# Attention over graph edges with a software gather: dropping implied semaphore waits, building the one-hot tile before the clip, and copying the edge rows after the query rows

## What is computed

```python
Q_h = (x @ Wq + bq).reshape(N, H, D)
K_h = (x @ Wk + bk).reshape(N, H, D)
V_h = (x @ Wv + bv).reshape(N, H, D)
E = (edge_attr @ We + be).reshape(-1, H, D)
score = K_h[src] * Q_h[dst] / sqrt(D) * E
score = exp(clip(score.sum(-1, keepdims=True), -5.0, 5.0))
wV = segment_sum(V_h[src] * score, dst)
Z  = segment_sum(score, dst)
out = layernorm(x + (wV / (Z + 1e-6)).reshape(N, H * D))
```

## Time and profile before

| | |
|---|---|
| median of three runs | 1276.63 us (1275.21 to 1278.20) |
| profiled execution, own time | 1267.1 us |
| its span | 1265.2 us |
| mean granted TensorE clock | 0.723 of full speed |
| busy: POOL, PE, PE weight load, DVE, ACT | 758.5, 694.1, 477.0, 620.3, 180.9 us |
| indirect DMAs of line 377 | 750, 0.97 us each |

### The profile page before, as it was taken

The page is one execution under the profiler, slowest core; times in us unless marked ns, Lnnn a source line. Parts: engine busy times, 40 slices in busy tenths (PEclk is TensorE's granted clock), DMA queues, the critical chain, the costliest instruction groups (busy, mean ns, idle before and its releaser), DMA issues.

```text
span 1265.2 us, 11863 instructions
## 1 busy us (share of the span) xinstructions
PE 694.1 (55%) x3376; PEld 477.0 (38%) x3376; DVE 620.3 (49%) x1205; ACT 180.9 (14%) x343; POOL 758.5 (60%) x788
## 2 busy tenths in 40 slices
PE   4655646454445446436585575575545555565554
PEld 4554333243234324324353333343324333343332
DVE  1221435454355346436594554554545544544556
ACT  1224201111011011101120110110111110110111
POOL 7371456666656656656536566666666666666660
PEclk8657767768667767767796776677676786687777
DMA  7464254354355345444455445445435454454440
GB/s 185 156 198 139 79 149 128 102 158 130 105 142 139 106 127 150 115 125 127 135 144 146 125 114 157 127 115 156 126 105 164 129 140 133 127 135 135 121 115 28
DMA packets 89940, 165.51 MB, mean 131 GB/s; under 512 B 43315, under 2 KB 61908, under 8 KB 86840
## 3 DMA queue, kind: packets, MB, share of 16 engines
q1 hardware_dynamic: 52843, 89.34, 25.6%
q0 software_dynamic: 37024, 75.35, 21.4%
HBM read 152.22 MB, written 12.39 MB: 130 GB/s over the span
## 4 chain that ended last, share of the span: by engine, by line
another core or an unknown queue 40%; PE 21%; issue 17%; DVE 13%; ACT 6%; DMA 2%; SPq 0%; DVEq 0%
PE psE L434 7%; DVE qe L786 5%; ACT qe L601 5%; PE psA L496 4%; PE psT L451 4%; DVE logit L875 2%; DMA xt<-xT 1%; DVE msg L890 1%; PE psQ L416 1%; DVE qke L866 1%; PE psA L461 1%; PE psE L404 1%; DVE clipped L881 1%; DVE ob L838 1%
## 5 line engine op out<-in xcount | busy, mean ns | idle before, releaser
L377 POOL DMA_INDIRECT kv<-kv_table,idx x750 | 726.7, 969 | 468.7 <-issue 221.4
L496 PE MATMUL psA<-place,msg 128*104 128x104 f32 x1564 | 210.4, 301 | 289.9 <-DVE msg L890 220.6
L496 PEld LDWEIGHTS psA<-place,msg 128*104 128x104 f32 x1564 | 198.5, 213 | 318.6 <-DVE msg L890 235.0
L434 PE MATMUL psE<-ea,we 97*96 97x512 f32 x392 | 256.3, 790 | 0.0
L774 DVE TENSOR_TENSOR place<-psI,rel_tile 128x832 f32<-128x832 f32 (+1 forms) x99 | 98.5, 995 | 293.9 <-remote 293.9
L451 PE MATMUL psT<-identity,qe 96*128 96x96 f32 x782 | 114.7, 307 | 153.0 <-DVE qe L786 124.0
L601 ACT ACTIVATE qe<-psE 96x1024 f32<-96x1024 f32 (+1 forms) x99 | 99.9, 1009 | 622.0 <-remote 469.4
L786 DVE TENSOR_TENSOR qe<-psQ,qe 96x1024 f32<-96x1024 f32 (+1 forms) x99 | 119.1, 1203 | 82.3 <-ACT qe L601 33.8
L451 PEld LDWEIGHTS psT<-identity,qe 96*128 96x128 f32 x782 | 96.9, 181 | 165.1 <-DVE qe L786 128.3
L866 DVE TENSOR_TENSOR qke<-psT,kv 128x768 f32<-128x768 f32 (+1 forms) x99 | 92.9, 938 | 87.6 <-remote 86.9
L434 PEld LDWEIGHTS psE<-ea,we 97*96 97x96 f32 x392 | 75.8, 218 | 79.3 <-issue 79.3
(11 more groups left out here) (107 smaller groups left out, 356.8 us busy)
## 6 DMA issues: line engine op xcount, KB each, us to landing
ea<-eaT SPq DMA_DIRECT2D x49, 768.0 KB
q_parts<-rel_table SPq DMA_DIRECT2D x24, 1008.0 KB
kv<-kv_table,idx POOLq DMA_INDIRECT x750
qwin<-q_table SPq DMA_DIRECT2D x198, 23.6 KB
xb<-xrows SPq DMA_DIRECT2D x24, 144.0 KB
out<-ob SPq DMA_DIRECT2D x24, 144.0 KB
q_table<-q_parts SPq DMA_DIRECT2D x4, 720.0 KB
kv_table<-kv SPq DMA_DIRECT2D x2, 960.0 KB
```

The source lines that it names most:

```text
L377: pool.indirect_dma_start(kv[:, k, t], None, kv_table, sources).then_inc(kv_in[k], 16)
L434: last = nc.tensor.matmul(psE[0:D, h, 0:size], we[:], ea[:, k // 2 % 2, edge:edge + size], start=True, stop=True)
L496: last = nc.tensor.matmul(psA[0:ML, off:off + PW], msg[:, s, t], place[:, s, t], start=opens, stop=closes)
```

## The change

All edits are inside `edge_pass`. The semaphore `e_done` goes. ACT's copy of `psE` waits for `q_done` of the group in place of `e_done` (and of `t_done`). Waits are dropped on PE (`qe_done` ahead of `to_edges`, and `ea_in` for the second group of a pair), on ACT (`t_done`, `sum_done`) and on DVE (`q_done` in `make_pick` and `make_qe`, `wt_done` before the clip, `sum_done` before `msg`, `rel_in` for three groups of four). `make_place` of g+1, which stood behind the clip of g, now stands ahead of it, behind `between(1)`; its own wait for `sum_done` of g-1 stays.

```diff
                         g = U * r + k
                         spans_of = [...]
-                        pe.wait_ge(ea_in[k // 2 % 2], 16 * lap(r, k, 4))
-                        if at >= 1:
-                            pe.wait_ge(qe_done, g)
+                        if k % 2 == 0:
+                            pe.wait_ge(ea_in[k // 2 % 2], 16 * lap(r, k, 4))
                         for h, size in spans_of:
                             edge = (k % 2) * GE + h * GE // 2
-                            last = nc.tensor.matmul(
+                            nc.tensor.matmul(
                                 psE[0:D, h, 0:size], we[:], ea[...], start=True, stop=True)
-                        last.then_inc(e_done, 1)
                         pe.wait_ge(qwin_in[k % QRING], 32 * lap(r, k, QRING))
...
-                        act.wait_ge(e_done, g + 1)
-                        if at >= 2:
-                            act.wait_ge(t_done, g - 1)
+                        act.wait_ge(q_done, g + 1)
                         nc.scalar.activation(qe[...], psE[...], ACT.Copy).then_inc(e_up, 1)
...
                             act.wait_ge(clip_done, g + 1)
                             nt = tiles(at)
-                            if at >= 2:
-                                act.wait_ge(sum_done, g - 1)
                             nc.scalar.activation(msg[...], clipped[...], ACT.Exp).then_inc(wt_done, 1)
...
-                        g = U * r + k
-                        dve.wait_ge(rel_in[k // BG % 2], 16 * (r + k // U + 1))
-                        if at >= 2:
-                            dve.wait_ge(q_done, g - 1)
+                        if k % BG == 0:
+                            dve.wait_ge(rel_in[k // BG % 2], 16 * (r + k // U + 1))
                         nc.vector.tensor_scalar(pick[...], rel[...], query_id[0:QR], None,
...
-                        dve.wait_ge(q_done, g + 1)
                         dve.wait_ge(e_up, g + 1)
                         nc.vector.tensor_tensor(qe[...], psQ[...], qe[...], ALU.mult).then_inc(qe_done, 1)
...
                         between(1)
-                        if at >= 2:
-                            dve.wait_ge(wt_done, g - 1)
+                        if at + 1 < NG:
+                            make_place(r, k + 1, at + 1)
                         dve.wait_ge(logit_done, g + 1)
                         nc.vector.tensor_scalar(clipped[...], logit[...], -5.0, 5.0, ALU.max,
                                                 ALU.min).then_inc(clip_done, 1)
                         between(2)
-                        if at + 1 < NG:
-                            make_place(r, k + 1, at + 1)
                         between(3)
-                        if at >= 2:
-                            dve.wait_ge(sum_done, g - 1)
                         dve.wait_ge(wt_done, g + 1)
                         nc.vector.tensor_tensor(msg[...], kv[...], msg[...], ALU.mult).then_inc(msg_done, 1)
```

More of the change, by code:

```diff
@@ L174, in gnn_program @@
         window_up, acc_out = sem("window_up"), sem("acc_out")
-        e_done, q_done, sum_done = sem("e_done"), sem("q_done"), sem("sum_done")
+        q_done, sum_done = sem("q_done"), sem("sum_done")
         pick_done, place_done = sem("pick_done"), sem("place_done")
```

## The result

The changed kernel takes 1288.29 us (median of six, 1285.34 to 1293.68), the kernel before 1277.47 us (six, 1275.21 to 1281.24). The ratio is 1.0088, 95% interval 1.0062 to 1.0115: slower by 11 us. Forecast were 1290 us. The profiled execution of the changed kernel took 1293.7 us by its own time and is the slowest of its six; that of before, with 1267.1 us, lies under all six of its own. Between the two profiles lie 26.6 us, of which less than half is the change.

The account below looks back on a forecast made before the run. POOL's gathers and stops were taken to bound the kernel. Terms of 10.2, 0.6, 1.2 and 1.0 us gave 13.0 us slower, 1289.7 us by the median (prediction 1290); range 1253 to 1303, the main forecast's own 1284 to 1303.

Parts of the forecast that it names:

- What bounds the kernel: POOL's gathers: 10.2 us a group of eight, compute under 6; only what lengthens or shortens POOL's stops moves the end.
- the forecast's floor: POOL's gathers without stops: 91 groups behind the ring's first eight take 928 us of the 1267.
- `place` ahead of the clip: At POOL's stops, clip and exponential come between release and `msg`: 17 stops at 0.6 us, 10.2 us slower.
- The number of stops: POOL's stops behind `msg`, 205 to 616 us: stay at 16, growing from 4.46 to about 5.1 us each.
- The waits at zero: Dropped waits on PE, ACT and DVE: records lie beside work, taken as 0, at most 0.6 us gain.
- the copy at zero: ACT's copy behind the query rows: 0.4 to 0.8 us later, hidden behind POOL or the burst, taken as 0.
- Behind group 48: 23 stops waiting for `q_done`: DVE's new order adds nothing, taken as 0, upper bound 14 us.
- The tail: Behind the last gather: three small groups lose the exponential's cover, about 1 us slower.
- The standstill: 630 to 652 us, POOL still and DVE full: four groups lose the exponential's cover, 1.2 us slower.
- Rival B: PE posts a quarter fewer signals, so POOL's stops shorten by 37 us: 1253 us, faster; chance 0.26.
- Rival D: Copy waiting for `q_done` is caught by holds, 3.1 us a stop, in half the stops: 1350 us; chance 0.11.

Follow-up runs that it names:

- h1: Kernel before with only the one-hot tile of the next group built ahead of the clip, on a chip with holds: 1301.86 us, ratio 1.0148.
- h2: Changed kernel with the one-hot tile put back behind the clip, on a chip with holds: 1304.21 us, ratio 1.0111 to the kernel before.
- c2: Kernel before without the implied waits, copy still on `e_done`, tile behind the clip, on a chip with holds: 1286.56 us, ratio 1.0106.
- the earlier limit: Kernel before with POOL's extra wait for `q_done` from group 12 on instead of 48, on a chip with holds: 1258.99 us, ratio 0.9881.

## Why the prediction was right, and where it wasn't

*What bounds the kernel: right.* POOL's pace and its stops. On the chip without holds the stops are gone and the time is 1056 us; the forecast's floor is what is left (group 8 starts at 107 us in the run with the tile alone, 928 us later POOL's last gather ends, at 1035).

*`place` ahead of the clip: mechanism and price right, its share wrong.* I put 17 stops at 0.6 us. (The count leaves out the stop of the earlier trace rows, whose gather at 619.41 lies behind the window; it should have been 18.) Measured are 0.51 us (1.45 against 0.94), and 0.8 where a longer step of the block lies between, as at 243.63 to 245.37. But only ten of the 14 stops in the first stretch are not of the new kind. They last 5.12 us on average in place of 4.46, as forecast (about 5.1), and account for 6.6 of the 18.5 us by which POOL's stops grew there. Four of the new kind, 9.67 us with the issue, account for 20.9, and two stops fewer give 8.9 back. I didn't have this part in this form.

*The number of stops: the failed step.* I wrote that I'd be wrong if it changed. It did, from 16 to 14, in the first stretch, with 24 gathers ahead of some. I treated each stop as a fixed event that an edit lengthens. The traces show more of a coupling. In the profile of before, of the 33 sums from 205 to 616 us 15 end 2.9 us behind a restart of POOL, and their signal rises 0.01 us later. Nearly all the others (16) end 7 us or more behind the restart, and their signals rise only 0.9 to 2.9 us after POOL has ended its last gather and stands still. So the hold doesn't merely happen to end near a stop; it ends with it, and a stop costs that delay and then DVE's chain. In the changed kernel, as far as the rises are recorded (85 of 99), only 3 of 32 sums have their signal within 0.1 us: the hold often catches the first one behind a restart too. My reading, which no run isolates, is that two rhythms meet: how far compute gets after a release before the next hold, and how far POOL gets until the ring is full. In the profile of before they lock into one stop in 16 gathers; in h1, h2 and c2 runs of 24 are frequent, each time by another edit, in c2 with no added work at all. The kernel before as it stands has only that one profile with holds, of an execution faster than all six.

*The waits at zero, the copy at zero: wrong on a chip with holds.* The waits alone are 1.1% on one chip, with the copy 1.1% on another. The argument (records of 21 to 51 ns beside work) is right about the records, as 0.998 on the chip without holds shows, and misses what they do to POOL's stops. (The rows on `msg` show a wait's record hidden beside running work; what an increment costs they don't show.) So the forecast's 13 us and the measured 11 agree, but by a sum whose terms are not the parts' own effects: singly the tile costs 1.5%, the waits 1.1% and the waits with the copy 1.1%, and all together 0.9%. That the total was hit is in part luck.

*Behind group 48: right.* 566.4 and 565.8 us, and 563.4 in the second profile of the changed kernel; the order of tile and clip isn't in stops that end with `q_done`. The tail is 0.6 us longer, where 1.0 was forecast.

*The standstill: right by luck.* I had 1.2 us, for four groups of DVE; group 46 to 48 takes 1.3 more. But before POOL stops there twice (4.7 and 22.0 us) and after it once (28.4), and in the second profile of the changed kernel that stretch is 5.3 us longer, with a stop of 32.4.

*Rival B (fewer signals, shorter stops): no sign of it.* The time rose, and so did the time in POOL's stops, with one signal a group fewer. The mean lateness of `sum_done` reads 4.9 us before and 6.9 after, the latter from the incomplete record, so it may be too high. The holds of `place` did get shorter than the 10 to 13 us that I forecast (7.8 us), but others stand at `qke`. *Rival D (the copy is caught)* was given 0.11 and is seen in four stops: in the one shown it takes 4.48 us from the copy to `msg` in place of 1.45 from `place`, so 3.0 us more, as it was priced (3.1). The stop as a whole grows by about 4.5, as the release comes later too (the copy starts 3.7 to 3.9 us behind the end of POOL's last gather). It is a tenth of the stops, not half; and it needs no copy on `q_done`, as h1 shows.

What stays open: why PE's signals come late while POOL issues, and why they do on some chips and not on another. What brings the first signal behind a restart into the hold, and so the runs of 24 gathers. And what in a dropped wait moves the rhythm; no run takes the waits one by one, and the copy alone was run only on the chip without holds.

## What to carry to other kernels

When two engines are coupled by a ring and the stops come in a regular pattern, first ask what keeps the pattern regular: an edit that costs nothing by its rows can change it, and single edits need not add up to the whole. Order the work behind a late signal so that as little as possible stands between it and the engine that sets the pace; better still, let that engine wait for the signal itself, as the earlier limit does (1.2% here). And before explaining a per cent by an edit, run the same pair on another chip.

## What the runs showed of the hardware

The same program takes 1056 us on one chip and 1275 to 1279 us (medians) on others, beyond any spread within a chip (1048 to 1059 in 32 runs on the one, 1269 to 1287 on the others). The difference is in the times at which PE's semaphores rise: 0.01 us behind the matmul's recorded end on the one (`sum_done`); on the others they can be 15 us late and come in bursts, while POOL issues its indirect DMAs back to back. (The profile models the end of a matmul; but the groups concerned last 0.6 to 1.9 us.) POOL issues them on the one chip as well, with no such effect. In before's profile the signals of matmuls recorded some 4 us apart (601.8 to 606.1 us) rise within 0.2 us of each other (617.23 to 617.42), 2.8 to 3.0 us behind the end of POOL's last gather. SP is slow on these chips too: one of its checks of a register takes 18 ns on average on the one chip, 81 ns in the first profile of before; there three in the hold around 605 us take 367 to 689 ns, and in the standstill from 630 to 652 us all take 18. The way from DVE to ACT shows nothing of it: the exponential starts 0.04 us or less behind the end of the clip in all 99 groups of before. The mean granted clock of TensorE was 0.793 of full speed in the run with the tile alone on the one chip, and 0.723 and 0.745 in before's first profile and in the later one of the changed kernel, with the holds; PE is busy for 251.8 of the 411 us from 205 to 616 us in the run with the tile alone, and for 203.2 in before's first profile.
